# Cross attention in rounds of four heads over two key tiles, with one maximum operation a head and six batches to a loop body

## The chip, the core and the metric

The kernel runs on one core of a Trainium2 chip. The metric is the time of one execution on the device in microseconds (us), over the whole program. TensorE (PE) multiplies matrices, VectorE (DVE) and ScalarE (ACT) work on vectors, GpSimd (POOL) does a few small vector operations, and SyncE (SP) issues most of the transfers (DMAs). Each engine runs its own instructions in the order in which they are written. Engines wait for each other only through semaphores.

## What is computed

A decoder layer in three stages on x (32 batches, 100 rows, 256 columns): self attention, cross attention to a context of 1444 rows, and a feed-forward block. The change is in the second stage alone, whose reference is, with its weights cut:

```python
def _w8a8_linear(x, w, b):                       # rows of x and w rounded to 8 bits, with a scale each
    qx, sx = _dyn_quant(x)
    qw, sw = _quant_weight(w)
    return jnp.einsum('bnc,oc->bno', qx, qw) * (sx * sw[:, 0]) + b

q = _w8a8_linear(x, wq, bq)                      # 16 heads of 16
k = cond @ wk.T + bk                             # cond: 32 x 1444 x 256
v = cond @ wv.T + bv
scores = jnp.einsum('bhnd,bhld->bhnl', q, k) * inv_sqrt_d + mask[:, None]
attn = jax.nn.softmax(scores, axis=-1)
o = jnp.einsum('bhnl,bhld->bhnd', attn, v)
return _w8a8_linear(o, wo, bo)                   # then residual and layer norm
```

## The kernel before

`cross_attention` walks through the 32 batches. The 1444 keys are 12 tiles of 128 (the last has 36), the 16 heads are four groups of four. A **unit** is one group and one key tile, so a batch has 48 (`UNITS`). For unit u, PE writes four score products into one of two PSUM banks (`ca_unit0`, `ca_unit1`, L1283), ACT takes the exponential of 400 columns into `ca_prob` (L1098), and PE, two units later (`LAG = 2`), multiplies it with the values into `ca_acc` (`weighted_values`, L1246). When the last unit is through, DVE copies `ca_acc` to `ca_oT` (L1435): one such copy a batch.

Between the units stand **tasks**, put there by hand with `place(u, ...)`. They belong to the next batch, unless said otherwise:

- `ct`: PE turns a third of the context (L1210) into a bank of the ring (`ca_ring0`, `ca_ring1`, used in turn), ACT copies it (L1047).
- `ka`, `kp`: PE makes a third of the keys for one half of the columns (L1129). ACT rounds it to bf16 (L1056), DVE takes the rest (L1347) and so frees the ring's bank, `km` on ACT rounds the rest (L1063), POOL takes what is left (L1002). When all six are through, SP stacks the three parts into `ca_ks` (L887: 12 and then 12 DMAs; L893 and L895 repeat rows already stacked) with waits between. `stacked[0]` is counted up when heads 0 to 7 lie there, `stacked[1]` for heads 8 to 15.
- `va`, `vp`: PE makes the values of two tiles (L1136), DVE adds the bias (L1362).
- `qq`, `qx`, `qp`, `qs`: the queries, quantised on DVE, split on POOL (L1009 to L1017), turned on PE (L1233), copied by ACT (L1074).
- `mh`, `ml`: PE writes a head's scores over 1024 keys and over the other 420 into `ca_rowmax` (L1163: two banks and one, with semaphores of their own, `ca_top_freed0` and `ca_top_freed1`), DVE adds the mask and takes the maximum (L1388, an operation for each). Heads 0 to 7 come late in the turn before their batch's own, heads 8 to 15 early in their own. After every fourth head, DVE splits the maxima (L1397 to L1402), and in `mr` PE turns them (L1172) into a unit's bank, from which ACT copies them into rows of `ca_qs` (L1081), so that the score product subtracts the maximum.
- `ma`, `mf`: the mask's largest value, which decides whether the mask is added.
- `eo`, `ex`, `ey`: the end of the batch before. `eo` turns `ca_oT` into `ca_rowmax` and DVE divides and quantises; `ex` turns that; `ey` is the output product (L1196), after which DVE adds and normalises (L1421 to L590), POOL takes the inverse root (L596) and DVE applies it (L603).

`Banks` gives each tile in a bank its turn: `wait_empty` waits until the bank's last reader is through, `wait_full` until it is written, `wait_out` until this tile has been read. `run_turns` runs the first batch straight, then a loop whose body holds two batches, then the last batch.

## Time and profile before

| | |
|---|---|
| median of 3 runs | 4172.97 us (4169.5 to 4175.27) |
| the profiled execution | 4178.84 us, of it 4177.0 us in the span from the first to the last instruction |
| busy: PE, DVE, ACT, POOL | 3662.6, 2444.9, 1735.0, 760.7 us (88, 59, 42, 18% of the span) |
| granted TensorE clock, mean | 0.925 |
| cross attention | from about 971 to 3555 us of the span |

A busy share is a mean over three stages, and the change touches one. So what counts is what PE waits for inside a batch of that stage.

### The profile page before, as it was taken

How to read it: one execution, taken by the hardware profiler on the slowest of the kernel's cores; microseconds unless marked ns; L12 is line 12 of the kernel's file. 1: busy time of each engine (PE TensorE's matmuls, PEld its weight loads, DVE VectorE, ACT ScalarE, POOL GpSimd, SP SyncE). 2: the span in 40 equal slices, each digit the busy share in tenths (PEclk: the TensorE clock that was granted, in tenths of full speed). 3: DMA queues.
4: the chain of work that ended last, by engine and by line, in shares of the span. 5: the costliest groups of instructions: out<-in, count | busy, mean ns of one | idle time of the engine just before them, and what ended most of it. 6: DMA issues, size and time to landing. Idle time of an engine off the chain costs nothing. (4 is left out here: it accounts for less than half of the span.)

```text
span 4177.0 us, 96840 instructions
## 1 busy us (share of the span) xinstructions
PE 3662.6 (88%) x34308; PEld 2589.7 (62%) x34308; DVE 2444.9 (59%) x5717; ACT 1735.0 (42%) x3500; POOL 760.7 (18%) x785
## 2 busy tenths in 40 slices
PE   7999999994988889889899898888888898688787
PEld 6999999882555555555555555555555554466666
DVE  4444444444666666666666666666666674555553
ACT  3232223231544444444444444444444443444443
POOL 0000000003110110110110110110110110366565
PEclk9999999996999999999999999999998996699998
DMA  2000000004464464364364364364364351100000
GB/s 93 13 12 12 12 12 9 3 9 102 76 103 81 77 108 82 75 109 82 73 109 85 73 111 83 73 108 85 73 108 86 73 91 28 56 17 13 25 9 21
DMA packets 122028, 257.80 MB, mean 62 GB/s; under 512 B 18880, under 2 KB 99392, under 8 KB 118512
## 3 DMA queue, kind: packets, MB, share of 16 engines
q1 hardware_dynamic: 115968, 247.34, 31.3%
q8 instruction: 317, 5.19, 0.6%
q10 hardware_dynamic: 5616, 4.23, 0.4%
q14 instruction: 127, 1.04, 0.1%
HBM read 99.72 MB, written 9.83 MB: 26 GB/s over the span
## 5 line engine op out<-in xcount | busy, mean ns | idle before, releaser
L1388 DVE CUSTOM_DVE_ANT_0 ca_rowmax<-ca_rowmax,ca_msk 100x1024 f32<-100x1024 f32 (+1 forms) x1024 | 926.8, 924 | 477.4 <-PE ca_rowmax L1163 469.2
L1098 ACT ACTIVATE ca_prob<-ca_unit 128x400 f32<-128x400 f32 (+1 forms) x1536 | 759.9, 502 | 832.5 <-PE ca_unit L1283 810.4
L1163 PE MATMUL ca_rowmax<-ca_ks,ca_qs 96*100 96x512 bf16 (+1 forms) x1536 | 515.8, 405 | 168.2 <-DMA ca_ks<-ca_ks 86.9
L1283 PEld LDWEIGHTS ca_unit<-ca_qs,ca_ks 99*128 99x128 bf16 (+1 forms) x6144 | 413.4, 102 | 280.9 <-issue 177.4
L1002 POOL TENSOR_TENSOR ca_key_part<-ca_key_rest,ca_key_part 128x512 bf16<-128x512 f32 (+1 forms) x192 | 210.0, 1100 | 2033.9 <-ACT ca_key_part L1063 2033.9
L1246 PE MATMUL ca_acc<-ca_prob,ca_vaug 128*17 128x100 f32 x12288 | 577.5, 262 | 0.0
L1283 PE MATMUL ca_unit<-ca_qs,ca_ks 99*128 99x100 bf16 (+1 forms) x6144 | 568.8, 215 | 1.3 <-issue 0.3
L1136 PE MATMUL ca_ring<-ca_wvT,ca_ctxT 128*128 128x256 f32 (+1 forms) x1536 | 440.7, 418 | 0.4 <-DVE ca_vaug L1362 0.4
L1129 PE MATMUL ca_ring<-ca_ctxT,ca_wkT 128*128 128x512 f32 (+1 forms) x768 | 364.9, 599 | 3.7 <-DVE ca_key_rest L1347 1.9
L1163 PEld LDWEIGHTS ca_rowmax<-ca_ks,ca_qs 96*100 96x100 bf16 x1536 | 156.7, 128 | 335.2 <-issue 225.9
L1136 PEld LDWEIGHTS ca_ring<-ca_wvT,ca_ctxT 128*128 128x128 f32 (+1 forms) x1536 | 295.8, 201 | 83.6 <-issue 27.7
L1246 PEld LDWEIGHTS ca_acc<-ca_prob,ca_vaug 128*17 128x17 f32 x12288 | 205.7, 96 | 139.7 <-issue 14.9
L1347 DVE SCALAR_TENSOR_TENSOR ca_key_rest<-ca_ring,ca_bk_col,ca_key_part 128x512 f32<-128x512 f32 (+1 forms) x192 | 137.7, 717 | 189.4 <-ACT ca_key_part L1056 189.4
L313 ACT ACTIVATE sa_capped<-sa_ps 100x400 f32<-100x400 f32 x128 | 64.7, 505 | 402.3 <-PE sa_ps L419 402.3
L1056 ACT ACTIVATE ca_key_part<-ca_ring,ca_bk_col 128x512 bf16<-128x512 f32 (+1 forms) x192 | 127.1, 662 | 244.1 <-PE ca_ring L1129 244.1
L1210 PE MATMUL ca_ring<-ca_ident,ca_ctx 128*128 128x128 f32 (+1 forms) x768 | 138.7, 305 | 86.5 <-issue 83.4
L1129 PEld LDWEIGHTS ca_ring<-ca_ctxT,ca_wkT 128*128 128x128 f32 x768 | 140.6, 198 | 108.3 <-issue 103.5
L259 POOL TENSOR_SCALAR_AFFINE_SELECT sa_causal<-sa_prob 100x400 f32<-100x400 f32 x128 | 69.6, 544 | 701.7 <-ACT sa_prob L320 701.7
L1210 PEld LDWEIGHTS ca_ring<-ca_ident,ca_ctx 128*128 128x128 f32 (+1 forms) x768 | 98.3, 153 | 133.6 <-issue 121.8
L86 PE MATMUL sa_ps<-sa_xT_hi,sa_w_hi 128*128 128x400 f32 x512 | 177.3, 346 | 0.0
L88 PE MATMUL sa_ps<-sa_xT_hi,sa_w_lo 128*128 128x400 f32 x512 | 175.1, 342 | 0.0
L87 PE MATMUL sa_ps<-sa_xT_lo,sa_w_hi 128*128 128x400 f32 x512 | 174.4, 341 | 0.0
(282 smaller groups left out, 6232.0 us busy)
## 6 DMA issues: line engine op xcount, KB each, us to landing
ca_ks<-ca_key_part SPq DMA_DIRECT2D x768, 90.2 KB, 4.1
ca_ks<-ca_ks SPq DMA_DIRECT2D x64, 722.0 KB, 5.8
ca_ctx<-in_ctx SPq DMA_DIRECT2D x32, 1408.0 KB
ca_ks<-ca_ks SPq DMA_DIRECT2D x64, 361.0 KB, 8.8
ca_msk<-in_mask_BxSxS_ff SPq DMA_DIRECT2D x32, 564.1 KB
sa_w_stage<-in_L_attn_w_qkv SPq DMA_DIRECT2D x12, 512.0 KB, 5.2
sa_x_in<-in_x ACTq DMA_DIRECT2D x8, 400.0 KB
sa_x_res<-in_x SPq DMA_DIRECT2D x8, 400.0 KB
```

The lines of the kernel that those rows point to most:

```text
L86: pe.matmul(out, w_hi, x_hi, start=(start and n == 0), stop=False)
L87: pe.matmul(out, w_hi, x_lo, start=False, stop=False)
L88: last = pe.matmul(out, w_lo, x_hi, start=False, stop=(stop and n == len(pairs) - 1))
L1002: pool.tensor_tensor(key_part[:, 2, c, s], key_rest[:, n % 2, 0:w], key_part[:, 1, c, s], ALU.subtract).then_inc(parts_out, 1)
L1098: act.activation(prob[0:rows(t), u % 3, :], unit[bank][0:rows(t), 0:QUAD * N], ACT.Exp)\
L1129: return pe.matmul(ring[bn.bank(task)][:, 0:w], wkT_s[:, ci, c * P:(c + 1) * P], ctxT[:, ci, s], start=(ci == 0), stop=(ci == C - 1))
L1136: last = pe.matmul(ring[bn.bank(task)][0:rows(t), j * D:(j + 1) * D], ctxT[:, ci, t * TL:t * TL + rows(t)], wvT_s[:, ci, :], start=(ci == ...
L1163: last = pe.matmul(rowmax[0:N, s0:s1], qs[0:STACK, par, h, :], ks[0:STACK, par, h, s0:s1], start=True, stop=True)
L1210: last = pe.transpose(tile[:, n * TL:n * TL + rows(t)], ctx_t[0:rows(t), t, c * P:(c + 1) * P], ident[0:rows(t), 0:rows(t)])
L1246: last = pe.matmul(acc[32 * j:32 * j + DH + 1, g * N:(g + 1) * N], vaug[0:rows(t), par, t, head_at(g * QUAD + j), :], prob[0:rows(t), u % ...
L1283: return pe.matmul(unit[bank][0:rows(t), j * N:(j + 1) * N], ks[:, par, h, s], qs[:, par, h, :], start=(j == 0), stop=True, skip_group_che ...
L1388: dve.tensor_tensor_reduce(rowmax[0:N, s0:s1], rowmax[0:N, s0:s1], msk[:, par, s0:s1], 1.0, -3.0e38, ALU.add, ALU.max, top[:, bank, h:h + ...
```

## The change

- **Rounds.** Two units become one round: one group of four heads over a pair of key tiles. The two banks are now one tensor `ca_unit` with one pair of semaphores. PE writes eight score products, ACT takes one exponential of 2x400 columns (two operations of 400 for the pair with the short tile), and PE multiplies with the values of the round before. For the last round that falls behind the first score products of the next batch, and the copy to `ca_oT` with it. Pairs of `ca_prob` are two, not three.
- **One maximum a head.** `mh` and `ml` become `mx`: three products in a row into three banks, one DVE operation over 1444 columns, one semaphore pair for all of `ca_rowmax`. The maxima are split and turned after every eighth head, now through `ca_rowmax` too.
- **Tasks** stand in a new table, `slots`, of 24 rounds. `ey` is cut in two: the apply step (L603) is the task `ez`, a round later.
- **The loop's body** holds six batches and runs five times. It held two and ran fifteen times.
- The quantise steps write in place, without `ca_x_sc`.

The core of the diff:

```diff
-    UNITS = NQ * TILES
-    LAG = 2
+    PAIRS = TILES // 2
+    ROUNDS = NQ * PAIRS
     HALF = EARLY = H // 2
...
-    place(1, ("eo",), ("ka", 0, 0), ("kp", 0, 0))
...
-    place(4, ("ka", 0, 1), ("kp", 0, 1), ("ey",))
...
-    place(27, ("mh", 0))
...
-    place(29, ("ml", 0), ("mh", 1), ("vp", 3))
...
+    BODY = 6
...
+    def pair_of(r):
+        g, k = divmod(r, PAIRS)
+        return g, (2 * k, 2 * k + 1)
...
+    slots = {
+        0: (("ct", 0, 0), ("ct", 0, 1), ("mx", 8)),
+        1: (("eo",), ("ka", 0, 0), ("kp", 0, 0)),
+        2: (("mx", 9), ("ka", 0, 1), ("kp", 0, 1), ("km", 0, 0)),
+        3: (("ex",), ("ct", 1, 0), ("ct", 1, 1), ("ka", 1, 0), ("km", 0, 1)),
+        4: (("kp", 1, 0), ("ey",), ("mx", 10), ("qq",), ("ka", 1, 1)),
+        5: (("ez",), ("kp", 1, 1), ("km", 1, 0), ("ct", 2, 0), ("ct", 2, 1), ("mx", 11)),
+        6: (("km", 1, 1), ("qx",), ("ka", 2, 0), ("kp", 2, 0)),
+        7: (("mx", 12), ("ka", 2, 1), ("kp", 2, 1), ("km", 2, 0), ("qp",)),
+        8: (("km", 2, 1), ("mx", 13), ("va", 0)),
+        9: (("mx", 14), ("vp", 0)),
+        10: (("mx", 15), ("qs", 0), ("va", 1)),
+        11: (("qs", 1), ("vp", 1), ("mr", 1)),
+        12: (("ma",), ("va", 2)),
+        13: (("mx", 0), ("vp", 2)),
+        14: (("mx", 1), ("va", 3)),
+        15: (("mx", 2), ("vp", 3), ("mf",)),
+        16: (("mx", 3), ("va", 4)),
+        17: (("mx", 4),),
+        18: (("mx", 5), ("vp", 4)),
+        19: (("mx", 6), ("va", 5)),
+        20: (("mx", 7),),
+        21: (("vp", 5),),
+        22: (("mr", 0),),
+        23: (),
+    }
...
-        unit = [ctx.enter_context(nc.psum_tensor(f"ca_unit{k}", [P, 512], F32)) for k in range(2)]
+        unit = ctx.enter_context(nc.psum_tensor("ca_unit", [P, 2, 512], F32))
...
-        bc = Banks(nc, sems, "ca_cur", cur_order, lambda t: cur_order.index(t) % 2)
-        bm = Banks(nc, sems, "ca_top", top_order + low_order, lambda t: int(t[0] == "ml"), lag={t: 1 for t in end_tasks})
+        bu = Banks(nc, sems, "ca_unit", [("u", r) for r in range(ROUNDS)], lambda t: 0)
+        bm = Banks(nc, sems, "ca_top", top_order, lambda t: 0, lag={t: 1 for t in end_tasks})
...
-        prob = sb("prob", [TL, 3, QUAD * N])
+        prob = sb("prob", [TL, 2, 2, QUAD * N])
...
-            with eng.Fori(0, B // 2 - 1) as pair:
-                turn(2 * pair + 1, 1)
-                turn(2 * pair + 2, 0)
+            with eng.Fori(0, (B - 2) // BODY) as body:
+                for n in range(BODY):
+                    turn(BODY * body + (n + 1), (n + 1) % 2)
             turn(B - 1, 1, last=True)
-            for n in range(EARLY):
-                skip(("mh", n), B)
-            for task in end_tasks:
-                do_task(B - 1, 1, task)
+            do_round(B, 0, ROUNDS)
...
+                _, tiles = pair_of(r)
+                bu.wait_full(act, ("u", r), b)
+                if not (isinstance(b, int) and ROUNDS * b + r < 2):
+                    act.wait_ge(pv_done, ROUNDS * b + (r - 1))
+                if rows(tiles[1]) == TL:
+                    act.activation(prob[:, r % 2], unit[:, :, 0:QUAD * N], ACT.Exp).then_inc(bu.freed[0], 1)
+                else:
+                    act.activation(prob[:, r % 2, 0], unit[:, 0, 0:QUAD * N], ACT.Exp)
...
-                if kind in ("mh", "ml"):
+                if kind == "mx":
                     h = task[1]
-                    if kind == "mh" and h == 0:
+                    if h == 0:
                         bn.wait_all_out(pe, [("qs", 0), ("qs", 1)], b)
-                    if kind == "mh" and h % HALF == 0:
+                    if h % HALF == 0:
                         pe.wait_ge(stacked[h // HALF], STACKED * (b + 1))
                     bm.wait_empty(pe, task, b)
-                    for s0, s1 in pieces(kind):
+                    for s0 in range(0, S, 512):
+                        s1 = min(s0 + 512, S)
                         last = pe.matmul(rowmax[0:N, s0:s1], qs[0:STACK, par, h, :], ks[0:STACK, par, h, s0:s1],
                                          start=True, stop=True)
-                    last.then_inc(bm.filled[bm.bank(task)], 1)
+                    last.then_inc(bm.filled[0], 1)
...
+                    pe.wait_ge(top_done, 2 * b + task[1] + 1)
+                    for j in range(HALF):
+                        last = pe.transpose(rowmax[:].bitcast(BF16)[STACK:FULL, j * N:(j + 1) * N],
+                                            top_part[:, task[1] * HALF + j, :], ident_b[0:N, 0:N])
+                    last.then_inc(bm.filled[0], 1)
...
+                if r < ROUNDS:
+                    g, tiles = pair_of(r)
+                    if r == 0:
+                        if isinstance(b, int) and b == 0:
+                            pe.wait_ge(ones_set, 2)
+                        bn.wait_out(pe, ("mf",), b)
+                        pe.sem_inc(pe_passed, 1)
+                        masked[par] = pe.value_load(mask_flag[:, par:par + 1].bitcast(I32))
+                    if g % 2 == 0 and tiles[0] == 0:
+                        bm.wait_out(pe, ("mr", g // 2), b)
+                    bu.wait_empty(pe, ("u", r), b)
+                    def head(n, j):
+                        h, t = g * QUAD + j, tiles[n]
+                        return pe.matmul(unit[0:rows(t), n, j * N:(j + 1) * N], ks[:, par, h, t * TL:t * TL + rows(t)],
+                                         qs[:, par, h, :], start=(j == 0), stop=True, skip_group_check=True)
+                    for n in range(2):
+                        head(n, 0)
+                    with pe.If(masked[par] != 0):
+                        for n, t in enumerate(tiles):
+                            pe.matmul(unit[0:rows(t), n, 0:QUAD * N], msk[:, par, t * TL:t * TL + rows(t)], eye4,
+                                      start=False, stop=True, skip_group_check=True)
+                    for n in range(2):
+                        for j in range(1, QUAD):
+                            last = head(n, j)
+                    last.then_inc(bu.filled[0], 1)
+                if 0 < r < ROUNDS:
+                    weighted_values(b, par, r - 1)
+                elif not (isinstance(b, int) and b == 0):
+                    weighted_values(b - 1, 1 - par, ROUNDS - 1)
...
-                    dve.tensor_tensor_reduce(rowmax[0:N, s0:s1], rowmax[0:N, s0:s1], msk[:, par, s0:s1], 1.0, -3.0e38,
-                                             ALU.add, ALU.max, top[:, bank, h:h + 1]).then_inc(bm.freed[bank], 1)
-                    if kind == "ml" and h % QUAD == QUAD - 1:
-                        g = h // QUAD
-                        bm.wait_out(dve, ("mh", h), b)
+                    dve.tensor_tensor_reduce(rowmax[0:N, 0:S], rowmax[0:N, 0:S], msk[:, par, :], 1.0, -3.0e38,
+                                             ALU.add, ALU.max, top[:, h:h + 1]).then_inc(bm.freed[0], 1)
+                    if h % HALF == HALF - 1:
                         bm.wait_out(dve, task, b)
-                        hs = slice(h - QUAD + 1, h + 1)
-                        chain = Chain(dve, top_step, NQ * b + g, 4)
-                        chain.link(dve.tensor_tensor(top[:, 0, hs], top[:, 0, hs], top[:, 1, hs], ALU.max))
-                        chain.link(dve.tensor_scalar(top_part[:, hs, 0], top[:, 0, hs], -1.0, None, ALU.mult))
-                        chain.link(dve.scalar_tensor_tensor(top_rest[:], top[:, 0, hs], -1.0, top_part[:, hs, 0],
+                        hs = slice(h - HALF + 1, h + 1)
+                        chain = Chain(dve, top_step, 2 * b + h // HALF, 3)
...
+                elif kind == "ez":
                     dve.wait_ge(out_stored, 16 * b + 1)
                     layernorm_apply(dve, summed, moments, rstd, res, 1, rstd_done, out_ready, b)
...
```

POOL, in the loop's body, the key parts (`ca_key_part`, one row for each of the first of six) and the inverse root (`ca_rstd`) of the batch before. Before:

```order
L1002 TENSOR_TENSOR ca_key_part<-ca_key_rest,ca_key_part 128x512 [waits ca_mid_out]
L1001 REGISTER_ALU
L1002 TENSOR_TENSOR ca_key_part<-ca_key_rest,ca_key_part 128x512 [waits ca_mid_out]
L596 TENSOR_TENSOR ca_rstd<-ca_var_eps,ca_minus_half 100x1 [waits ca_moments_done]
L1001 REGISTER_ALU
```

And in the changed kernel:

```order
L982 TENSOR_TENSOR ca_key_part<-ca_key_rest,ca_key_part 128x512 [waits ca_mid_out]
L981 REGISTER_ALU
L982 TENSOR_TENSOR ca_key_part<-ca_key_rest,ca_key_part 128x512 [waits ca_mid_out]
L981 REGISTER_ALU
L982 TENSOR_TENSOR ca_key_part<-ca_key_rest,ca_key_part 128x512 [waits ca_mid_out]
L596 TENSOR_TENSOR ca_rstd<-ca_var_eps,ca_minus_half 100x1 [waits ca_moments_done]
```

The third key part now stands ahead of the inverse root. That third part waits for the task `km` of (1, 0).

DVE, around the apply step of the batch before (L603, `ez`) in the changed kernel:

```order
L637 TENSOR_SCALAR ca_x_int<-ca_x_q 100x256 [waits ca_q_step]
L1402 ISA
L603 TENSOR_SCALAR ca_res<-ca_summed,ca_moments,ca_rstd 100x256 [waits ca_rstd_done,ca_out_stored]
L1323 REGISTER_ALU [waits ca_parts_out]
L1324 SCALAR_TENSOR_TENSOR ca_key_rest<-ca_ring1,ca_bk_col,ca_key_part 128x512 [waits ca_hi_out]
```

The rest of the keys of (1, 1), which frees `ca_ring1`, now stands behind the apply step, and so behind POOL's inverse root.

PE, the products of (1, 1) and the context's third third, in round 5. In the changed kernel:

```order
L1111 MATMUL ca_ring1<-ca_ctxT,ca_wkT 128x512
L1192 MATMUL ca_ring0<-ca_ident,ca_ctx 128x128 [waits ca_next_freed0]
L1192 MATMUL ca_ring0<-ca_ident,ca_ctx 128x128 x2
L1192 MATMUL ca_ring0<-ca_ident,ca_ctx 128x36
L1192 MATMUL ca_ring1<-ca_ident,ca_ctx 128x128 [waits ca_next_freed1]
L1192 MATMUL ca_ring1<-ca_ident,ca_ctx 128x128 x2
L1192 MATMUL ca_ring1<-ca_ident,ca_ctx 128x36
L1146 MATMUL ca_rowmax<-ca_ks,ca_qs 100x512 [waits ca_top_freed0]
L1146 MATMUL ca_rowmax<-ca_ks,ca_qs 100x512
L1146 MATMUL ca_rowmax<-ca_ks,ca_qs 100x420
```

The transposes into `ca_ring1` need the bank that the key product, four transposes earlier, has just filled. Before, two units, a `mr` and a `mh` stood between. Of the maxima, three products follow one wait for all of `ca_rowmax`, where before the two parts of a head waited for banks of their own.

## Rows read from the trace of the kernel before

**Rows 1.** Timeline of PE: start, length, operation, count.

```profile
2042.91 0.35 PE L1283 MATMUL ca_unit<-ca_qs,ca_ks 99*128 99x100 bf16 x4
2043.19 0.37 PE L1246 MATMUL ca_acc<-ca_prob,ca_vaug 128*17 128x100 f32 x8
2043.49 0.38 PE L1163 MATMUL ca_rowmax<-ca_ks,ca_qs 96*100 96x420 bf16 x1
2043.71 1.03 PE L1136 MATMUL ca_ring<-ca_wvT,ca_ctxT 128*128 128x256 f32 x4
2044.57 0.35 PE L1283 MATMUL ca_unit<-ca_qs,ca_ks 99*128 99x100 bf16 x4
```

**Rows 2.** Window: length; busy us of PE, PEld, DVE, ACT, POOL; clock; DMA.

```profile
1173.45:1178.80 5.35, 5.35 (x32) 3.10 (x33) 1.29 (x2) 1.01 (x2) 0.00 (x0) 0.50 0.59 88
```

**Rows 3.** Timeline of DVE: the copies that end three batches in a row.

```profile
1513.42 0.57 DVE L1435 COPY ca_oT<-ca_acc 128x400 f32<-128x400 f32 x1
...
1588.54 0.57 DVE L1435 COPY ca_oT<-ca_acc 128x400 f32<-128x400 f32 x1
...
1669.77 0.57 DVE L1435 COPY ca_oT<-ca_acc 128x400 f32<-128x400 f32 x1
```

**Rows 4.** Waits of the whole span: total us, times, longest.

```profile
PEld ca_rowmax L1163 <- DVE ca_top L1388: 92.4, 106, 2.6
...
PE ca_rowmax L1163 <- DMA ca_ks<-ca_ks: 86.9, 29, 4.2
...
PE ca_ring L1210 <- issue: 83.4, 28, 4.2
```

**Rows 5.** Timeline of PE where the next batch follows without a jump.

```profile
1985.15 0.82 PE L1163 MATMUL ca_rowmax<-ca_ks,ca_qs 96*100 96x512 bf16 x3
...
1987.81 1.88 PE L1129 MATMUL ca_ring<-ca_ctxT,ca_wkT 128*128 128x512 f32 x4
```

**Rows 6.** Timeline of PE where the loop jumps back.

```profile
2070.02 3.43 PE L1129 MATMUL ca_ring<-ca_ctxT,ca_wkT 128*128 128x512 f32 x4
```

**Rows 7.** Groups by form: busy us, mean ns, idle before.

```profile
L1388 DVE CUSTOM_DVE_ANT_0 ca_rowmax<-ca_rowmax,ca_msk 100x1024 f32<-100x1024 f32 x512 | 633.1, 1237 | 333.3 <-PE ca_rowmax L1163 330.3
...
L1388 DVE CUSTOM_DVE_ANT_0 ca_rowmax<-ca_rowmax,ca_msk 100x420 f32<-100x420 f32 x512 | 313.3, 612 | 144.1 <-PE ca_rowmax L1163 138.9
...
L1782 ACT ACTIVATE ff_soft<-ff_soft 100x800 f32<-100x800 f32 x64 | 55.2, 862 | 43.9 <-POOL ff_soft L1677 43.8
```

**Rows 8.** Timeline of all engines: from a key product to the apply step.

```profile
2077.42 0.38 PE L1196 MATMUL ca_rowmax<-ca_woT,ca_x_intT 128*100 128x256 bf16 x2
...
2078.34 0.75 DVE L1347 SCALAR_TENSOR_TENSOR ca_key_rest<-ca_ring,ca_bk_col,ca_key_part 128x512 f32<-128x512 f32 x1 [3.25 <-ACT ca_key_part L1056]
...
2079.01 0.47 DVE L1421 SCALAR_TENSOR_TENSOR ca_summed<-ca_rowmax,ca_o_st,ca_step_row 100x256 f32<-100x256 f32 x1
...
2079.78 0.63 ACT L1063 ACTIVATE ca_key_part<-ca_key_rest 128x512 bf16<-128x512 f32 x1
...
2080.49 1.16 POOL L1002 TENSOR_TENSOR ca_key_part<-ca_key_rest,ca_key_part 128x512 bf16<-128x512 f32 x1 [3.49 <-ACT ca_key_part L1063]
...
2081.61 0.55 POOL L596 TENSOR_TENSOR ca_rstd<-ca_var_eps,ca_minus_half 100x1 f32<-100x1 f32 x1
...
2082.28 0.41 DVE L603 TENSOR_SCALAR ca_res<-ca_summed,ca_moments,ca_rstd 100x256 f32<-100x256 f32 x1 [0.80 <-POOL ca_rstd L596]
```

**Rows 9.** Timelines of ACT and SP: last key third, and its stacking.

```profile
2011.37 0.61 ACT L1056 ACTIVATE ca_key_part<-ca_ring,ca_bk_col 128x420 bf16<-128x420 f32 x1 [1.32 <-PE ca_ring L1129]
...
2012.17 10.67 SPq L887 DMA_DIRECT2D ca_ks<-ca_key_part  x16
...
2025.80 0.59 SPq L895 DMA_DIRECT2D ca_ks<-ca_ks  x1
```

**Rows 10.** Timeline of PE: head 0 waits for its keys, in two batches.

```profile
1173.45 1.09 PE L1163 MATMUL ca_rowmax<-ca_ks,ca_qs 96*100 96x512 bf16 x2 [3.36 <-DMA ca_ks<-ca_ks]
...
2034.95 0.63 PE L1163 MATMUL ca_rowmax<-ca_ks,ca_qs 96*100 96x512 bf16 x2 [2.09 <-DMA ca_ks<-ca_ks]
```

200 lines of the change are left out of this document (59 added, 141 removed).

## The prediction

> **What bounds the kernel now.** I read the busy times first, then the copies that end each batch, then what PE waits for, then PE's timeline through two batches. PE is busy through 88% of the span, so what counts is PE's own work and its waits. A batch is over when DVE copies the accumulator. One batch in two takes 75.1 us (1588.54 less 1513.42), the next 81.2 us (1669.77 less 1588.54) [rows 3]. The 6.1 us more come from the loop's jump: at each jump PE's first transposes wait twice for nothing that the profile shows, 28 waits and so 14 jumps, 83.4 us together, 6.0 us a jump [rows 4]. The clock falls with it: the first four key products after a jump take 3.43 us, without one 1.88 us [rows 5, 6].
>
> Inside a batch PE waits for two things: for DVE to free the banks of the maxima (92.4 us over the stage, 3.0 us for each of 31 batches) and for the stacked keys of head 0 (86.9 us, 2.8 us a batch) [rows 4]. The rest is work. So a batch of 75.1 us has some 69 us in which PE works, part of it at the low clock: behind a wait of 3.36 us PE ran 5.35 us at a granted clock of 0.50, which is 1.2 GHz [rows 2, 10].
>
> **The prices.** A unit's four score products hold PE for 0.28 us (2043.19 less 2042.91), the product with the values 0.30, a half of a value pair 0.86 (2044.57 less 2043.71) [rows 1]. Three maximum products in a row last 0.82 us; the last alone lasts 0.38 and holds PE for 0.22, so the three hold it for 0.66 [rows 1, 5]. A DVE maximum takes 1.24 us over 1024 columns and 0.61 over 420 [rows 7]: 1.03 ns a column, so 1.67 us over 1444, and 0.06 more until the result is out. ACT's exponential over 800 columns takes 0.86 [rows 7]. From the end of a product to the start on ACT or DVE I take 0.2 us, and 0.1 the other way.
>
> **What goes.** Ten of 14 jumps: 10 x 6.1 = **61 us**. The two old kinds of wait: 5.8 us a batch, since each stands in the list of new ones again under its new size. PE's work falls a little: 24 changes from score products to value products instead of 48, and no second start for 16 maxima. The 0.28 us of four score products holds about 0.09 that I put down to the change of kind. That would be 2.2 us and 0.5 us for the maxima, 2.7 at most, zero at least; I take **2.3**.
>
> **What comes.** A round's period alone is no loss. Eight score products, 0.2, the exponential 0.86 and 0.1 make about 1.7 us, and a round with a maximum has 1.16 + 0.66 = 1.8 us of work for PE. The waits come where tasks stand closer together than their chains are long. A wait is the chain's length less PE's work meanwhile:
>
> - a. *Round 3, `ka` (1, 0)* right behind `ct` (1, 1): ACT has two context copies and `ex` to do. About **1.2**.
> - b. *Round 4, maximum of head 10* right behind `ey`. All of `ca_rowmax` is one buffer now, and DVE reads `ey` behind the rest of the keys. In the trace DVE is through 2.06 us (2079.01 + 0.47 - 2077.42) after the key product ends [rows 8]. Less 0.22 for `ey`: **1.9**.
> - c. *Round 5, `ct` (2, 1)*. It needs `ca_ring1`, freed by DVE's rest of the keys (1, 1). On DVE that stands behind `ez`, which waits for POOL's root, and on POOL the root stands behind the third key part, which waits for ACT's `km` (1, 0), which stands behind `kp` (1, 1) of this round. From the end of PE's key product: ACT 0.2 + 0.6, `km` 0.63, POOL's key part 1.12 until the next starts, root 0.55, 0.12, apply and rest of keys 0.3 + 0.75, to PE 0.1 [rows 8]. With a lag of 0.1 at POOL that is 4.5 us, less 0.49 for `ct` (2, 0): **4.0**. In the kernel before the apply step waited 0.80 us for POOL and no bank hung on it [rows 8].
> - d. *Round 1, `eo`* behind the maximum of head 8: one maximum is 0.82 + 0.2 + 1.73 + 0.1 = 2.85 us from one head's products to the next use of the bank, PE has 0.66 + 1.16 to do: **1.0**.
> - e. *Round 10, `qs` 0 and `va` 1*: the queries' split on POOL, with two key parts ahead of it, comes about 0.9 late, and the value product needs the bank that ACT copies 800 columns from: 0.2 + 0.86 + 0.1. Together **2.0**.
> - f. *Round 12*: the score products of head 8 need ACT's copy of eight heads' maxima, and `mr` stands right in front: 0.2 + 0.86 + 0.1, **1.1**.
> - g. *Round 13, head 0*. Its keys are stacked by SP: sixteen DMAs in 10.67 us, a wait, two more. From ACT's rounding of the last third to head 0's product it was 23.6 us (2034.95 less 2011.37) [rows 9, 10]. No step of that is changed. In the new order PE has less in between: six rounds 6.9, three maxima 2.0, five value halves 4.3, small products 1.9, and the waits e and f, together 18.5 to 19. So **4.7**.
> - h. *Rounds 13 to 20*, eight maxima, a round each, in one buffer: seven intervals of at least 2.85 = 20.0 us, PE's work in them 7 x 1.82 + 6 x 0.86 = 17.9: **2.0**. DVE works off one maximum in 1.7 us, so it is not DVE's load but the single buffer.
> - i. *Rounds 22 and 0*: `mr` and its ACT copy ahead of the last exponential, on which the next batch's first score products wait: **0.9**.
>
> Sum **18.8 us**. The clock: c and g are waits of 4 us, such as [rows 10] shows ahead of 5.35 us at half rate [rows 2], which cost 2.7 us each. Before there was one a batch. So **2.7** more.
>
> **The sum.** A batch without a jump: 75.1 - 5.8 - 2.3 + 18.8 + 2.7 = 88.5 us, 13.4 more. Over 31 batches 415 us, less 61 for the jumps: +354. On the profiled execution's 4178.84 that is 4533 us. The median of the runs is 5.9 lower, so I say **4530 us**.
>
> For the range: c is at least 1.8 (POOL's key part and root taken out of its chain), g between 2.1 (the shorter of the two waits in [rows 10]) and 6, a to i together 12 to 22, the clock's part 0 to 5. A batch is then 79 to 94 us and the time about 4240 to 4700. The ends would need all terms to lean one way, so I say 4380 to 4680.
>
> **Rivals.**
>
> 1. *The waits are there, but smaller* (17%): a wait at c lets DVE and ACT catch up, so d, e, f are partly paid by it, and the clock doesn't fall more often than before. 12 us of waits and no clock term: 79.0 us a batch, +121 - 61, so about 4240; halfway between, 4380. For it speaks that waits in a chain often overlap; against it that the keys' chain (g) starts only after c.
> 2. *The clock stays low for long* (15%). From round 13 on PE stops in each round for 0.2 to 1 us. In the rows of before such short stops leave the clock at full rate. If it falls there, work of some 24 us takes up to twice as long, as the key products do in [rows 6] against [rows 5]; half of that stretch would give 8 us a batch and about 4780 us. The Trainium skill ("TensorE: Matmul & The Clock Gate", section "A second HAM failure mode: psum-queue depth-cycling") speaks for this: it tells of a kernel that went round PSUM banks with very short waits between groups of matmuls, and whose clock swung between its two levels. By that rule the low clock would not be tied to c and g alone; the rows of before, with waits of 0.2 to 0.9 us at full clock, do not bear it out.
> 3. *Faster* (4%). The removed jumps pay for everything. PE's fewer waits and less work give 5.8 + 2.3 = 8.1 us a batch, the jumps 2.0, so the point is 10.1 us a batch: if the nine waits and the clock sum to less, the kernel is faster; with 8 us it would be 4173 - 31 x 0.1 - 61, about 4110. The mechanism would be that one buffer for the maxima is enough, since DVE has time to spare. Against it: g alone, whose chain is unchanged, and c are 8.7.
> 4. *No difference* (1%): the same, at that point.
>
> The forecast itself has 63%, 4430 to 4640. Below 4380 I leave 12%, above 4680 another 10%. About 0.2% is what a measurement of this kernel can tell from no change. Faster by more than that 4%, within it 1%, slower 95%.
>
> **What the profile after should show.** A copy L1435's successor every 87 to 91 us, and 4 jumps. PE waits for DVE's rest of the keys ahead of a context transpose, about 4 us a batch, and DVE waits 2.5 us for POOL ahead of the apply step. PE waits for the stacked keys 4 to 5 us a batch. Maxima of heads 1 to 7 follow each other every 2.85 us, with PE stops in front. A granted clock below 0.925 in the mean. I am wrong if the context transposes don't wait, if the maxima follow PE's work and not DVE's, or if the clock is low outside of the stretches behind c and g.

## The result, and the profile after

The changed kernel takes **4531.14 us** in the median (4525.9 to 4539.55, 4 runs) beside 4171.24 us (4165.93 to 4175.27, 4 runs) for the kernel before, run on the same chip: a ratio of 1.086, 95% interval 1.0842 to 1.0882. The forecast was 4530 us. The profiled execution has a span of 4524.2 us and a mean granted clock of 0.909 (before 4177.0 us and 0.925).

The busy times at the head of the page, answering to those in the table of before: PE, the bound of both kernels, is busy for less time than before (3638.9 against 3662.6 us), in a span 347 us longer. DVE works less too. What was added is idle time of PE.

```profile
PE 3638.9 (80%) x34308; PEld 2651.1 (59%) x34308; DVE 2286.5 (51%) x4309; ACT 1630.2 (36%) x2796; POOL 759.4 (17%) x785
```

The copies of the accumulator, which answer to [rows 3] (timeline of DVE):

```profile
1936.51 0.57 DVE L1409 COPY ca_oT<-ca_acc 128x400 f32<-128x400 f32 x1 [3.10 <-PE ca_acc L1228]
2024.97 0.57 DVE L1409 COPY ca_oT<-ca_acc 128x400 f32<-128x400 f32 x1 [3.04 <-PE ca_acc L1228]
2113.04 0.57 DVE L1409 COPY ca_oT<-ca_acc 128x400 f32<-128x400 f32 x1 [3.09 <-PE ca_acc L1228]
2207.12 0.57 DVE L1409 COPY ca_oT<-ca_acc 128x400 f32<-128x400 f32 x1 [8.38 <-PE ca_acc L1228]
```

A batch without a jump takes 88.5 and 88.1 us, the one with the jump 94.1, and the one behind it still 91.5. There are four jumps. The waits of PE over the whole span answer to [rows 4] (total us, times, longest):

```profile
PE ca_rowmax L1146 <- DMA ca_ks<-ca_ks: 197.0, 32, 9.2
PE ca_ring L1192 <- DVE ca_key_rest L1324: 117.0, 33, 3.8
PE ca_rowmax L1146 <- DVE ca_top L1363: 98.8, 228, 2.0
PE ca_rowmax L1146 <- DVE ca_summed L1393: 52.7, 31, 1.7
```

And PE's timeline through one batch, of which only the rows that begin after a stop are shown here (the stop stands in brackets):

```profile
1940.05 0.65 PE L1163 MATMUL ca_rowmax<-ca_ident,ca_oT 128*100 128x128 f32 x4 [1.14 <-DVE ca_top L1363]
1948.93 1.12 PE L1111 MATMUL ca_ring<-ca_ctxT,ca_wkT 128*128 128x512 f32 x2 [1.00 <-ACT ca_ctxT L1027]
1953.90 0.81 PE L1146 MATMUL ca_rowmax<-ca_ks,ca_qs 96*100 96x512 bf16 x3 [1.74 <-DVE ca_summed L1393]
1961.99 0.73 PE L1192 MATMUL ca_ring<-ca_ident,ca_ctx 128*128 128x128 f32 x4 [3.71 <-DVE ca_key_rest L1324]
1976.25 0.81 PE L1146 MATMUL ca_rowmax<-ca_ks,ca_qs 96*100 96x512 bf16 x3 [0.64 <-DVE ca_top L1363]
1979.03 0.82 PE L1146 MATMUL ca_rowmax<-ca_ks,ca_qs 96*100 96x512 bf16 x3 [0.28 <-DVE ca_top L1363]
1981.13 1.13 PE L1118 MATMUL ca_ring<-ca_wvT,ca_ctxT 128*128 128x256 f32 x4 [0.92 <-ACT ca_qs L1054]
1986.27 0.74 PE L1254 MATMUL ca_unit<-ca_qs,ca_ks 99*128 99x100 bf16 x8 [0.99 <-ACT ca_qs L1060]
1996.43 1.44 PE L1146 MATMUL ca_rowmax<-ca_ks,ca_qs 96*100 96x512 bf16 x3 [6.95 <-DMA ca_ks<-ca_ks]
2003.69 0.81 PE L1146 MATMUL ca_rowmax<-ca_ks,ca_qs 96*100 96x512 bf16 x3 [0.28 <-DVE ca_top L1363]
2006.48 0.82 PE L1146 MATMUL ca_rowmax<-ca_ks,ca_qs 96*100 96x512 bf16 x3 [0.19 <-DVE ca_top L1363]
2012.05 0.82 PE L1146 MATMUL ca_rowmax<-ca_ks,ca_qs 96*100 96x512 bf16 x3 [0.94 <-DVE ca_top L1363]
2014.84 0.81 PE L1146 MATMUL ca_rowmax<-ca_ks,ca_qs 96*100 96x512 bf16 x3 [0.28 <-DVE ca_top L1363]
2017.62 0.82 PE L1146 MATMUL ca_rowmax<-ca_ks,ca_qs 96*100 96x512 bf16 x3 [0.28 <-DVE ca_top L1363]
2023.59 0.71 PE L1254 MATMUL ca_unit<-ca_qs,ca_ks 99*128 99x100 bf16 x8 [0.53 <-ACT ca_prob L1080]
```

From the top: d, a, b, c, two small stops and e, f, g, five stops of h, i. Every wait of the forecast is there, at its place and with its releaser, but for a half of e (see below). The rows from 2003.69 to 2017.62 show h: the maxima's products start every 2.79 us (one at 2009.27 began without a stop and isn't in the list), at the pace of DVE's maximum and the single buffer.

Wait c, seen from the engines it runs through (timeline of POOL and DVE, in order of time; PE's row at 1961.99 above is the next link):

```profile
1959.09 1.15 POOL L982 TENSOR_TENSOR ca_key_part<-ca_key_rest,ca_key_part 128x512 bf16<-128x512 f32 x1 [8.46 <-ACT ca_key_part L1043]
1960.20 0.55 POOL L596 TENSOR_TENSOR ca_rstd<-ca_var_eps,ca_minus_half 100x1 f32<-100x1 f32 x1
1960.87 0.41 DVE L603 TENSOR_SCALAR ca_res<-ca_summed,ca_moments,ca_rstd 100x256 f32<-100x256 f32 x1 [1.67 <-POOL ca_rstd L596]
1961.19 0.75 DVE L1324 SCALAR_TENSOR_TENSOR ca_key_rest<-ca_ring,ca_bk_col,ca_key_part 128x512 f32<-128x512 f32 x1
```

The root waits on POOL behind the third key part, DVE waits 1.67 us for it, the rest of the keys stands behind, and PE behind that. Wait g, in the rows of ACT and SP that answer to [rows 9]:

```profile
1972.16 0.61 ACT L1036 ACTIVATE ca_key_part<-ca_ring,ca_bk_col 128x420 bf16<-128x420 f32 x1 [2.22 <-PE ca_ring L1111]
1972.97 10.03 SPq L863 DMA_DIRECT2D ca_ks<-ca_key_part  x16
1985.61 0.59 SPq L871 DMA_DIRECT2D ca_ks<-ca_ks  x1
```

From ACT's rounding to head 0's product it is 24.3 us here (1996.43 less 1972.16). The batch shown is a long one: in 30 batches of this trace the chain takes 22.6 to 24.4 us, 23.4 in the mean, and 23.5 in the trace of the kernel before.

The clock, by windows of this trace (length; busy us of PE, PEld, DVE, ACT, POOL; granted clock; DMA): the first stretch lies behind c, the second between, the third behind g, the fourth runs from round 14 into round 3 of the next batch.

```profile
1963.61:1970.40 6.79, 6.79 (x57) 3.71 (x56) 2.38 (x3) 3.03 (x5) 1.15 (x1) 0.53 0.71 219
1970.50:1993.00 22.50, 16.12 (x205) 11.05 (x203) 12.04 (x18) 8.95 (x13) 4.69 (x6) 1.00 0.86 117
1996.43:2000.60 4.17, 4.17 (x27) 3.03 (x31) 2.28 (x3) 0.32 (x1) 0.00 (x0) 0.50 0.56 65
2001.00:2040.00 39.00, 34.20 (x430) 21.98 (x431) 22.65 (x38) 17.23 (x27) 2.31 (x2) 1.00 0.26 53
```

### The profile page after: what moved, and what is told of

Its sections match the earlier page's. It is cut to its first block and busy times, and to the rows that moved or that the text cites. A ratio compares the mean times of both kernels' runs of the same rounds, so it can differ in the third digit from the quotient of the medians.

```text
span 4524.2 us, 91165 instructions
## 1 busy us (share of the span) xinstructions
PE 3638.9 (80%) x34308; PEld 2651.1 (59%) x34308; DVE 2286.5 (51%) x4309; ACT 1630.2 (36%) x2796; POOL 759.4 (17%) x785
## 5 line engine op out<-in xcount | busy, mean ns | idle before, releaser
L1363 DVE CUSTOM_DVE_ANT_0 ca_rowmax<-ca_rowmax,ca_msk 100x1444 f32<-100x1444 f32 x512 | 855.0, 1670 | 761.0 <-PE ca_rowmax L1146 757.0
L1077 ACT ACTIVATE ca_prob<-ca_unit 128x800 f32<-128x800 f32 x640 | 534.7, 835 | 987.3 <-PE ca_unit L1254 986.1
L1146 PE MATMUL ca_rowmax<-ca_ks,ca_qs 96*100 96x512 bf16 (+1 forms) x1536 | 471.0, 420 | 348.5 <-DMA ca_ks<-ca_ks 197.0
L1254 PEld LDWEIGHTS ca_unit<-ca_qs,ca_ks 99*128 99x128 bf16 (+1 forms) x6144 | 392.1, 104 | 333.6 <-issue 226.3
L1254 PE MATMUL ca_unit<-ca_qs,ca_ks 99*128 99x100 bf16 (+1 forms) x6144 | 497.6, 220 | 69.8 <-ACT ca_qs L1060 32.6
L1146 PEld LDWEIGHTS ca_rowmax<-ca_ks,ca_qs 96*100 96x100 bf16 x1536 | 168.7, 136 | 511.4 <-issue 249.9
L1228 PE MATMUL ca_acc<-ca_prob,ca_vaug 128*17 128x100 f32 x12288 | 461.9, 266 | 1.9 <-issue 1.6
L1111 PE MATMUL ca_ring<-ca_ctxT,ca_wkT 128*128 128x512 f32 (+1 forms) x768 | 416.0, 657 | 34.1 <-ACT ca_ctxT L1027 33.0
L1228 PEld LDWEIGHTS ca_acc<-ca_prob,ca_vaug 128*17 128x17 f32 x12288 | 241.1, 99 | 101.2 <-issue 32.4
L1111 PEld LDWEIGHTS ca_ring<-ca_ctxT,ca_wkT 128*128 128x128 f32 x768 | 151.8, 217 | 131.3 <-issue 82.8
```

The lines of the kernel that those rows point to most:

```text
L1077: act.activation(prob[:, r % 2], unit[:, :, 0:QUAD * N], ACT.Exp).then_inc(bu.freed[0], 1)
L1111: return pe.matmul(ring[bn.bank(task)][:, 0:w], wkT_s[:, ci, c * P:(c + 1) * P], ctxT[:, ci, s], start=(ci == 0), stop=(ci == C - 1))
L1146: last = pe.matmul(rowmax[0:N, s0:s1], qs[0:STACK, par, h, :], ks[0:STACK, par, h, s0:s1], start=True, stop=True)
L1228: last = pe.matmul(acc[32 * j:32 * j + DH + 1, g * N:(g + 1) * N], vaug[0:rows(t), par, t, head_at(g * QUAD + j), :], prob[0:rows(t), r % ...
L1254: return pe.matmul(unit[0:rows(t), n, j * N:(j + 1) * N], ks[:, par, h, t * TL:t * TL + rows(t)], qs[:, par, h, :], start=(j == 0), stop=T ...
L1363: dve.tensor_tensor_reduce(rowmax[0:N, 0:S], rowmax[0:N, 0:S], msk[:, par, :], 1.0, -3.0e38, ALU.add, ALU.max, top[:, h:h + 1]).then_inc(b ...
```

## The experiments

All differences below are between medians, with the interval of the ratio to the kernel before in brackets. The runs were taken in four groups, in which the kernel before took 4171, 4173, 4174 and 4176 us, so a difference between kernels of two groups is good to some 5 us. For the kernels on which the argument rests, these are the 29 batches from the second copy of the accumulator to the last but one, in windows like those above. Kernel before with a body of six:

```profile
1199.33:3401.26 2201.93, 2016.16 (x22189) 1211.12 (x22185) 1486.78 (x3568) 1066.74 (x2146) 284.90 (x319) 0.95 0.51 91
```

The changed kernel:

```profile
1222.41:3820.12 2597.71, 2024.77 (x22186) 1283.90 (x22186) 1345.32 (x2291) 975.66 (x1509) 284.98 (x319) 0.90 0.43 77
```

Divided by 29, both with five batches in six free of a jump: 75.93 us a batch, PE busy 69.5 and idle 6.4, against 89.58, busy 69.8 and idle 19.8.

**The jumps alone** (`e1_before_body6`): the kernel before with six batches to a body.

```diff
-            with eng.Fori(0, B // 2 - 1) as pair:
-                turn(2 * pair + 1, 1)
-                turn(2 * pair + 2, 0)
+            with eng.Fori(0, (B - 2) // 6) as body:
+                for n in range(6):
+                    turn(6 * body + (n + 1), (n + 1) % 2)
```

> The kernel before with one part of the change alone: the loop's body holds six batches and runs five times. My theory prices the jump at 6.1 us and ten of 14 jumps go, all else stands as before: 61 us less than the kernel before, about 4110 us, 4 jumps left in the trace. Rival one: a jump's cost is partly the turn of the batch it stands in, and a body of six, three times as long, brings code loading inside the body; then less than 30 us are won, or none. Rival two: a longer body costs each jump more than a short one; then the gain lies between 30 and 55 us.

Measured: 4108.97 us (0.982 to 0.9863), 64 us less for ten jumps. PE's waits for nothing at a jump fell from 83.4 us, 28 times, to

```profile
PE ca_ring L1210 <- issue: 24.6, 8, 3.7
```

The jump's price stands, and this part of the change alone is a gain of 1.6%.

**The jumps given back** (`e2_after_body2`): the changed kernel with `BODY = 2` for `BODY = 6`.

> The changed kernel with its body set back to two batches, so that the rounds, the single maximum and the new order of tasks stand alone. My theory: the two parts of the change don't touch each other, so ten jumps come back at 6.1 us each and the time is 4531 + 61 = 4592 us, and the rounds and the order alone have cost about 420 us. Rival: in the changed kernel each jump is paid out of waits that PE has in the next rounds anyway (round 1's, 3's and 4's, 3.9 us together by the trace), so a jump costs only about 2 to 3 us and the time is about 4555 us.

Measured: 4599.04 us (1.0995 to 1.1043), 68 us more. The two parts of the change add up; the rival, that a jump is hidden in waits that PE has anyway, is out. So the rounds, the single maximum and the table of tasks cost 426 us by themselves (4599 less 4173).

**POOL's root first** (`e3_root_first`): on POOL alone, the root stands ahead of the third key part.

```diff
+                    if (k, c) == (1, 0) and not (isinstance(b, int) and b < 2):
+                        inverse_root(pool, rstd[:], var_eps[:], minus_half[:], moments_done, rstd_done, b - 2)
...
-                elif task[0] == "ey":
+                elif task[0] == "ey" and isinstance(b, int) and b >= B - 2:
```

> The changed kernel with one instruction moved on one engine: POOL's inverse root stands ahead of the third key part, as in the kernel before, and no longer behind it. My theory: wait c (PE ahead of the context's third third, 3.7 us a batch, 117 us in all in the trace) is made of DVE's wait for this root; with it gone, PE waits only for ACT's rounding and DVE's rest of the keys, about 1.4 us, and the stretch at half clock behind it goes too. That is 2.3 us a batch of wait alone (70 us, about 4460) or about 5 with the clock (155 us, about 4375); I expect 4370 to 4460, with the clock's part in it. Rival one: DVE's rest of the keys is late for another reason (the load of DVE, the output product), so that c stays above 3 us and the time within 20 us of 4531. Rival two: what c gives back is lost at round 4, 5 or 13, since the keys' stacking sets the batch; then c falls and the wait for the stacked keys grows by as much.

Measured: 4475.35 us (1.0694 to 1.0746), 56 us less; the expected range ended at 4460. The wait c fell, but to 2.8 us and not to 1.4, and in 26 of 29 batches the clock still fell to half behind it. The timeline of POOL and DVE shows why:

```profile
1950.08 0.55 POOL L596 TENSOR_TENSOR ca_rstd<-ca_var_eps,ca_minus_half 100x1 f32<-100x1 f32 x1 [5.19 <-DVE ca_var_eps L590]
...
1953.35 1.15 POOL L984 TENSOR_TENSOR ca_key_part<-ca_key_rest,ca_key_part 128x512 bf16<-128x512 f32 x1 [2.72 <-ACT ca_key_part L1045]
...
1953.37 1.29 DVE L603 TENSOR_SCALAR ca_res<-ca_summed,ca_moments,ca_rstd 100x256 f32<-100x256 f32 x1
```

The root is ready long before, yet the apply step now lasts 1.29 us, not 0.41: it began 0.02 us behind POOL's key part and ended some 0.15 us after it, and DVE's rest of the keys stands behind it. Until 1953.37 DVE was busy with the query's quantise steps.

**The repeat of rows first** (`e4_repeat_first`): on SP, the repeat of heads 0 to 7 no longer stands behind four transfers for heads 8 to 15.

```diff
                 put(0, (0, 1, 2))
-                put(1, (0,))
                 repeat(0)
-                put(1, (1, 2))
+                put(1, (0, 1, 2))
```

> The changed kernel with one group of four transfers moved on SP: the repeat of the rows for heads 0 to 7 is issued before the stacking of the first key part for heads 8 to 15, not behind it. My theory: wait g (head 0 for its stacked keys, 6.2 us a batch, 197 us in all in the trace) is the length of SP's chain, so it falls by about what those four transfers take on SP, some 2.5 us (four of sixteen in 10.7 us): 80 us, about 4450; with less clock loss up to 4400. Rival: SP's issue is not the limit and the transfers' flight is; then the repeat starts no earlier, g stays at 6 us and the time within 20 us of 4531. A third way: the second half's keys come too late for head 8's maximum; then g falls but a wait for the keys appears in the round of head 8, and nothing is won.

Measured: 4485.41 us (1.0707 to 1.0763), 46 us less. The wait g fell from 197.0 to

```profile
PE ca_rowmax L1145 <- DMA ca_ks<-ca_ks: 150.9, 32, 7.9
```

So SP's order is part of g, 1.4 us a batch where 2.5 was expected. The chain from ACT's rounding to head 0's product fell from 23.4 to 22.0 us in the mean: the last repeat is issued only 0.6 us earlier (medians, 12.9 for 13.5 us behind the rounding) and lands 0.5 us faster (8.8 for 9.3). What the other transfers and their waits hold of g wasn't tried.

**Filling the wait g** (`e5_fill_wait`): products that nobody needs, in front of head 0's.

```diff
-                    if h % HALF == 0:
-                        pe.wait_ge(stacked[h // HALF], STACKED * (b + 1))
                     bm.wait_empty(pe, task, b)
+                    if h == 0:
+                        for n in range(18):
+                            pe.matmul(rowmax[0:P, 0:D], wkT_s[:, 0, 0:P], wkT_s[:, 0, :], start=True, stop=True)
+                    if h % HALF == 0:
+                        pe.wait_ge(stacked[h // HALF], STACKED * (b + 1))
```

> The changed kernel with 18 more products on PE, of a constant weight matrix with itself (256 columns each, about 0.28 us each, 5.1 us together by the value products of the same size), into ca_rowmax right ahead of the wait g for head 0's keys; the real products write over them. PE is busy then where it stood still for 5.4 to 7 us, and nobody waits for the added work, which ends before the keys come. It measures the clock's term by itself. My theory: the low clock behind g comes from the wait, so it is gone. In the trace PE runs for some 4.2 us at half clock behind g; at full clock that is 2.1 us less a batch, 65 us in all: about 4466, and a mean granted clock near 0.94. Rival one: the clock behind g is low for another reason (the dense fp32 work, the transfers), so nothing changes: 4531 within 15. Rival two: the added products delay the keys' chain, by load on PE's queue or on the memory ports: slower than 4531.

Measured: 4515.06 us (1.0802 to 1.0838), 16 us less. The edit was mis-sized: an fp32 product is two instructions, so the 18 are 36 and last longer than the wait they fill (head 0's product comes 25.2 us behind ACT's rounding, in the mean, and not 23.4):

```profile
1985.07 8.04 PE L1144 MATMUL ca_rowmax<-ca_wkT 128*128 128x256 f32 x36
```

It doesn't price the clock, but a kernel with 7.9 us of needless work in each batch is no slower.

**Filling it to the right length** (`e9_fill_short`): `range(12)` for `range(18)`.

> The changed kernel with products of a constant matrix in the wait g, as before, but 12 of them and not 18. The 18 held PE for 7.9 us (36 instructions, 1985.07 to 1992.94), longer than the wait they were to fill (6.2 us a batch), and so gave 1.2 to 2 us a batch back; 12 are 24 instructions, 5.3 us by the same rows, which is less than the wait. My theory (the wait g lowers the clock, and the work behind it pays 2.1 us a batch): about 65 us less than the changed kernel, 4466, since nothing is delayed now, and a mean granted clock near 0.935. Rival: the low clock is worth no more than the 16 us that the longer fill gave, and 4515 comes again or more. The other way: filled to the end or not, PE still stands 1 us for the keys, and the clock falls all the same: 4531.

Measured: 4436.66 us (1.0601 to 1.0636), **94 us less** than the changed kernel, and a mean clock of 0.94. One batch on PE's timeline, the fill and what follows:

```profile
1968.04 5.45 PE L1144 MATMUL ca_rowmax<-ca_wkT 128*128 128x256 f32 x24
...
1974.06 0.81 PE L1149 MATMUL ca_rowmax<-ca_ks,ca_qs 96*100 96x512 bf16 x3 [0.57 <-DMA ca_ks<-ca_ks]
```

and the clock behind it, by a window:

```profile
1974.00:1980.00 6.00, 5.39 (x64) 3.90 (x65) 4.00 (x5) 1.67 (x2) 0.00 (x0) 1.00 0.65 88
```

The keys come no sooner (23.3 us behind ACT's rounding in the mean, 23.4 in the changed kernel). Work that serves nothing makes the kernel 2% faster, 3.0 us a batch, because more of the products run at 2.4 GHz and not at 1.2: in none of the 29 batches does the clock fall behind g, where it fell in all of them.

Not all of the 94 us belongs to g. Laid over PE's instructions, the clock records of the changed kernel's trace put 4.6 us a batch of PE's busy time behind g at 1.2 GHz, which cost 2.3 us, near the 2.1 of the expectation. The rest of the gain fits the low stretches behind c and at the jumps, which are shorter in this trace (PE's busy time in them 7.8 us a batch, 10.0 in the changed kernel). Why the fill shortens these isn't shown.

**The apply step early** (`e6_apply_early`): e3's kernel with `ez` ahead of `qq`.

```diff
-        4: (("kp", 1, 0), ("ey",), ("mx", 10), ("qq",), ("ka", 1, 1)),
-        5: (("ez",), ("kp", 1, 1), ("km", 1, 0), ("ct", 2, 0), ("ct", 2, 1), ("mx", 11)),
+        4: (("kp", 1, 0), ("ey",), ("mx", 10), ("ez",), ("qq",), ("ka", 1, 1)),
+        5: (("kp", 1, 1), ("km", 1, 0), ("ct", 2, 0), ("ct", 2, 1), ("mx", 11)),
```

> The kernel with the root ahead of the third key part, and the apply step (ez) one place earlier on DVE, ahead of the query's quantise steps. It asks why wait c fell only from 3.7 to 2.8 us there. In that trace the apply step lasts 1.29 us in place of 0.41, and it begins just as POOL's third key part does (1953.37 and 1953.35) and ends with it. My theory: the two hold each other up, and placed earlier, with POOL idle (0.7 us before its key part at least), the step takes 0.41 again, so that c falls by another 0.9 us to about 1.95: 27 us less than 4475, about 4448. Rival one: the step is long for its own reasons in this order (its operands were just written); then it stays at 1.29 us, and the time at 4475. Rival two: the quantise steps, now later, run into POOL's key part and are stretched instead; then c and the time stay.

Measured: 4476.08 us (1.0702 to 1.0741), as before the edit. The second rival came true: the apply step is back to 0.41 us, and the last quantise step, 0.29 us elsewhere, is caught in its place (timeline of POOL and DVE):

```profile
1951.31 1.15 POOL L984 TENSOR_TENSOR ca_key_part<-ca_key_rest,ca_key_part 128x512 bf16<-128x512 f32 x1 [2.72 <-ACT ca_key_part L1045]
1951.43 1.17 DVE L637 TENSOR_SCALAR ca_x_int<-ca_x_q 100x256 bf16<-100x256 f32 x1
```

**The quantise steps late** (`e10_quantise_late`): e6's kernel with `qq` behind `kp` (1, 1), in round 5.

> The kernel with root first and apply step early, and the query's quantise steps (qq) moved behind DVE's rest of the keys (1, 1). In the last trace the apply step was back to 0.41 us, but the last quantise step (L637, 0.29 us elsewhere) took 1.13, begun 0.1 us behind POOL's key part and ended with it, so that wait c stayed at 2.83 us. My theory: c is then a matter of DVE's queue alone, with this collision in it; with the quantise behind, the rest of the keys starts when ACT has rounded (ACT ends at 1950.71 in that trace), 1.8 us earlier, and c falls to about 1.0. That is 56 us of wait and, with c under 1.5 us, up to 1.5 us a batch of clock: 4476 less 56 to 100, so 4375 to 4420. Rival: DVE's rest is then held by something else, or the wait moves on to head 11's maximum or to the query's product, which needs the quantise: above 4455.

Measured: 4349.10 us (1.0395 to 1.043), 127 us less than e6's kernel, more than the 100 at the end of the range. The wait c:

```profile
PE ca_ring L1194 <- DVE ca_key_rest L1326: 34.8, 33, 1.1
```

It gives 51 us (from 85.9). PE's busy time fell as well, from 3619.7 to 3535.5 us, with the mean clock up from 0.913 to 0.932: at 1.05 us the wait no longer brings the half clock behind it. PE's row behind c in one batch, and the window from it on:

```profile
1987.93 0.73 PE L1194 MATMUL ca_ring<-ca_ident,ca_ctx 128*128 128x128 f32 x4 [1.06 <-DVE ca_key_rest L1326]
```

```profile
1987.93:1996.00 8.07, 8.07 (x95) 5.04 (x95) 5.92 (x12) 4.48 (x9) 2.07 (x2) 1.00 0.62 185
```

Behind c the clock is low in 2 of the 29 batches here, in 26 of e6's. That was worth more than the wait: 127 us less the 51 is 2.5 us a batch, where 1.5 at most was expected. Against the changed kernel the three edits together (e3, e6, e10) give back 182 us, half of the 360 that the changed kernel is slower, and all of it hung on the order on two engines.

**Two new tables** (`e7_new_table`, `e8_table_root`): every task is placed anew; both have SP's order of e4, the second POOL's order of e3. The core of the second:

```diff
-        3: (("ex",), ("ct", 1, 0), ("ct", 1, 1), ("ka", 1, 0), ("km", 0, 1)),
-        4: (("kp", 1, 0), ("ey",), ("mx", 10), ("qq",), ("ka", 1, 1)),
-        5: (("ez",), ("kp", 1, 1), ("km", 1, 0), ("ct", 2, 0), ("ct", 2, 1), ("mx", 11)),
-        6: (("km", 1, 1), ("qx",), ("ka", 2, 0), ("kp", 2, 0)),
+        3: (("km", 0, 0), ("ka", 1, 0), ("ex",), ("kp", 1, 0), ("ka", 1, 1), ("km", 0, 1), ("kp", 1, 1)),
+        4: (("ey",), ("ct", 2, 0)),
+        5: (("ct", 2, 1), ("km", 1, 0), ("km", 1, 1), ("qq",)),
+        6: (("ka", 2, 0), ("kp", 2, 0), ("mx", 10)),
...
+        10: (("ma",), ("ez",), ("qs", 0)),
```

> The changed kernel with another table of slots and the repeat of heads 0 to 7 first on SP; rounds, single maximum, body and all work are the same. The keys come one to two rounds earlier, key products stand apart from the context transposes, ez stands in round 10, head 0 in round 14, the eighth maximum still in round 21. My theory: the rounds cost nothing by themselves and all that was lost are the waits of the table and their clock. PE's work in a batch is some 67 to 69 us, with a, b, c, d, f gone and g below 3 us a batch takes 74 to 78 us, and the time is 4070 to 4200, at or under the kernel before. Rival: the rounds themselves cost (a single buffer for maxima, 800 columns of exponential in one go, bank pair shared), so that a batch stays above 80 us with any table, and the time above 4260.

> A second table of the same kind, on the kernel with POOL's root first and the repeat of heads 0 to 7 first. It tells whether the gain hangs on one lucky table. Expected like the other one, a batch of 74 to 78 us and 4070 to 4200 in all; its values come later and head 0 earlier, in round 13, so the wait for the stacked keys may be 1 to 2 us longer a batch. Rival as there: above 4260.

Measured: 4130.28 us (0.9878 to 0.9912) and 4076.65 us (0.9757 to 0.9797). The 29 batches of the first, then of the second:

```profile
1208.15:3429.83 2221.68, 1982.33 (x22186) 1254.02 (x22187) 1364.30 (x2291) 986.81 (x1508) 287.49 (x319) 0.93 0.49 90
```

```profile
1196.55:3355.65 2159.10, 1899.68 (x22186) 1221.61 (x22186) 1395.88 (x2291) 982.58 (x1509) 290.30 (x319) 0.97 0.50 93
```

PE is idle for 8.3 us a batch in the first and for 8.9 in the second, which is the faster one: busy 68.4 against 65.5 us, at a clock of 0.93 against 0.97. Both times lie in the expected range, and the rival (above 4260) is out. Beside e1, the kernel before with the same body, the first is 21 us slower and the second 32 us faster: 76.6 and 74.5 us a batch against 75.9. So with another table the rounds and the single maximum cost next to nothing against the kernel before, or gain a little.

That they cost nothing by themselves isn't shown. Both new kernels have SP's new order, the second POOL's too, and e1 doesn't have SP's: its trace has 95.2 us of waits for the stacked keys, the new tables' 1.3 and 4.9 us. The kernel before with a body of six and SP's new order was not run; it might be faster than e1.

**A body of ten** (`e11_best_body10`): the second table with `BODY = 10`, two jumps fewer.

> The second new table with a loop body of ten batches that runs three times, in place of six and five times: two jumps fewer. By 6.1 to 6.8 us a jump 12 to 14 us less than the kernel with six, about 4064. Rival: a body of ten batches makes each jump or the loading of code inside the body dearer, and the time stays at 4077 or rises.

Measured: 4053.78 us (0.9664 to 0.9751), 23 us less where 12 to 14 were expected; the runs spread over 37 us, so the excess is no finding. It is the fastest kernel of the study, 2.9% under the kernel before.

## Why the prediction was right, point by point

- **The sum.** A batch without a jump was forecast at 88.5 us; the copies show 88.1 and 88.5, and the mean of 29 batches less four jumps of 6.1 us is 88.7. The nine waits and the jumps, the mechanism, are shown. That the time came out within 1 us of the forecast is luck: two terms of the sum were 1.5 us too small (g, the clock), another 1.6 too small on the other side (PE's work), and the waits other than g 1.2 too large.
- **The jumps**, 6.1 us each: 6.4 in e1, 6.8 in e2.
- **The waits.** Forecast 18.8 us, found 19.1 (g from the waits of the whole span, 197.0 us over 32; e, h and i from the batch shown):

| wait | a | b | c | d | e | f | g | h | i |
|---|---|---|---|---|---|---|---|---|---|
| forecast, us | 1.2 | 1.9 | 4.0 | 1.0 | 2.0 | 1.1 | 4.7 | 2.0 | 0.9 |
| found, us | 1.0 | 1.7 | 3.7 | 1.1 | 1.8 | 1.0 | 6.2 | 2.0 | 0.5 |

- **g** was mis-sized by 1.5 us. Its chain was right: 23.6 us forecast, 23.4 found in the mean of 30 batches. PE has less to do in it than the 18.5 to 19 us that were put against it: 17.2 (23.4 less 6.2). A part of that is a slip in the adding: the terms as given, 6.9 + 2.0 + 4.3 + 1.9 and 3.1 for e and f, make 18.2, by which g would have been 5.4. Another is that a round takes PE less time than was reckoned (see below). The place and the cause of g were right; e4 shows that four of SP's transfers are in it.
- **e** came out in size, not in make: the 0.92 us of the value product is there, but the queries' split on POOL costs nothing (PE waits 3.0 us for it in the whole trace), and in its place stand two stops for heads 14 and 15 (0.64 and 0.28), a case of h before h.
- **c** was right, and its step by step account too, but one term: DVE waits 1.67 us for POOL, where 2.5 was forecast, since the quantise steps keep DVE busy for longer. e3 showed that the root's place is a part of it (32 us of 117), e10 that the quantise steps are the larger one. That the quantise steps, which stand ahead of the apply step in DVE's queue, hold `ca_ring1` too was not in the prediction.
- **PE's work and the clock.** Forecast: 2.3 us less work and 2.7 us more for the clock, together +0.4 of busy time. Found together: +0.3 (69.8 less 69.5), but each was larger. The clock records of the two traces, laid over PE's instructions in the 29 batches, put 14.4 us a batch of PE's busy time at 1.2 GHz, against 6.0 in e1: 8.4 us more at half rate, which cost 4.2. So the work itself fell by 3.9 us, more than the 2.7 that the prediction held for the most. The rows of a round show where: the eight score products and the sixteen value products hold PE for 0.92 us (1943.17 less 1942.25), where the prediction reckoned 1.16 less some 0.09 for the change of kind. In some rounds the score products hold PE longer; over all rounds at full clock the two take 1.02 us in the mean.

```profile
1942.25 0.52 PE L1254 MATMUL ca_unit<-ca_qs,ca_ks 99*128 99x100 bf16 x8
...
1943.17 0.82 PE L1146 MATMUL ca_rowmax<-ca_ks,ca_qs 96*100 96x512 bf16 x3
```

- **Where the clock is low.** Of PE's busy time at 1.2 GHz, some 4.6 us a batch lie behind g (4.5 in e1), and 7.4 behind c, where the prediction had put one more stretch of 5.35 (so 3.7 us of cost for 2.7). The other 2.6 us lie at the jumps and at the start of some batches, 14 stretches in 29 batches. So the last sign of being wrong, a low clock outside of the stretches behind c and g, is there in a small part; the prediction had seen it at the jumps.
- **The rivals.** Waits that hide each other (rival 1) did not come; eight of the nine stand at nearly their size or above it, i at 0.5 us for 0.9. The clock low for long through rounds 13 to 23 (rival 2) did not either: 1.00 from 2001 to 2040, through eight short stops. The Trainium skill's section on depth-cycling ("TensorE: Matmul & The Clock Gate", section "A second HAM failure mode: psum-queue depth-cycling") tells of a clock that swings with very short waits between groups of matmuls; the trace does not show it for this order of stops, but see below for the first new table. The gain of rival 3 needs waits and clock under 10.1 us a batch; the new tables have 8.3 and 8.9 us of idle time, jumps included, and both gain (1.0 and 2.2%), which agrees with that point.

What stays open: how the loss splits between the rounds and the single maximum was not tried. The waits b, d and h, 4.8 us a batch, stand in front of the single buffer of the maxima; the new tables say only that most of the loss as a whole can be placed away.

## What to carry to other kernels

When a tuned kernel is regrouped, its table of task places is part of the tuning: the same rounds and body cost 8.6% with one table and gain 2.2% with another (and two small reorders, on SP and POOL). Price the new waits chain by chain, through every queue that the moved instruction stands in, and add the clock behind each long one, some 2.3 to 3.7 us a batch here, beside waits of 2.8 to 6.2 us. And test parts of a change apart: the longer loop body was a gain of 64 us that the rest hid.
